# Layer norms of an eight-block network: the scaling of two tiles in every five moves from VectorE to GpSimd

## The chip, the cores and the metric

The kernel runs on one core of a Trainium2 chip, in one launch. The metric is device time in microseconds (us). The engines are TensorE (PE, its weight loads apart as PEld), VectorE (DVE), ScalarE (ACT), GpSimd (POOL) and SyncE (SP), which here issues most DMAs.

## What is computed

A network of eight blocks works on `x`, 128 graphs of 40 nodes with 128 features (5120 rows of 128 numbers, float32). Four blocks work on the graph (a graph convolution or attention within each graph), four are feed-forward (a token mixer with a scan, and three expert layers). Each block is fed with a layer norm of `x`, and its result is added to `x`:

```python
def _layernorm(x, axis=-1, eps=1e-05):
    m = jnp.mean(x, axis=axis, keepdims=True)
    v = jnp.var(x, axis=axis, keepdims=True)
    return (x - m) / jnp.sqrt(v + eps)
...
    x = x + _L1_gnn_ref(_layernorm(x, axis=-1), adj, nodemask, ...)
    x = x + _L1_ffn_ref(_layernorm(x, axis=-1), L1_ffn_gamma, L1_ffn_beta, ...)
```

The second feed-forward block (L1_ffn) takes a layer norm of its own input once more, with a gain and an offset, so there are nine rounds of norm in eight calls.

## The kernel before

`x` is kept turned, as features by rows (`XT`, 128 x 5120). `layer_norm` (line 178) is called eight times, here named by the prefix of its tiles: n0 (before L0_gnn), n1 (L0_ffn), n2 (L1_gnn), n3 (L1_ffn, two rounds), n5 (L2_gnn), n6 (L2_ffn), n7 (L3_gnn), n8 (L3_ffn). A call works on TT = 40 tiles of 128 rows by 128 features and has these steps:

- TensorE turns four tiles at a time into PSUM (`pin`, line 228), ScalarE copies them into `xt` (line 271). n0 and n5 have the rows already.
- VectorE takes `bn_stats` of each tile (`stats`, line 304), then the mean and variance of 20 tiles at once (`moments`, lines 310 to 317). It does so for both halves of 20 tiles before anything else. ScalarE takes the root (`rooted`, line 262).
- `apply` (lines 319 to 330) scales a half: a reciprocal of 128x20 numbers (line 322), a drain, and then 20 instructions `tensor_scalar` on 128x128 numbers (line 328), which subtract the tile's mean and multiply by its reciprocal deviation. Both are pointers to a column of `ms`, one number per row. After every fifth tile it raises `normed`.
- TensorE waits for `normed`, turns five tiles back (`back`, line 236) into one of two PSUM buffers `pout`, and ScalarE copies the 128x640 numbers into `XNP` (line 286, or 288 with gain and offset), then raises `out_copied`.
- With `slots` (n0, n2, n5, n7) TensorE also turns eight pairs of graphs for each five tiles (`turn`, line 247), and ScalarE copies them into `XNG` in two pieces (lines 293 and 296). n1, n3, n6 and n8 have no slots.

With `twice` (n3) the stats and `apply` run once over the raw rows without any of the steps on TensorE, and then again over the result. n3 and n8 also store the normed rows to DRAM (`SparseExperts.store`, `f_xn`, line 892), in two halves, each when `normed` has reached 4 and 8. In n1 the SP queue issues the 26 DMAs for the weights of the next block meanwhile (`load_weights`, line 2583), and GpSimd clears three small tiles. In n2 GpSimd clears some tiles and SP reloads. Otherwise GpSimd has nothing to do within a norm.

Every engine's part of a call is a straight program in order. The call ends with a barrier of all engines (line 184), and the next block's instructions start behind it.

Of the kernel before, what the change touches and what calls it, by code (L numbers as in the profile page):

```python
# [9 lines left out]
ALU = mybir.AluOpType  # L10
# [11 lines left out]
TT = T // 128  # L22
# [155 lines left out]
def layer_norm(nc, g, slots=False, name="ln", tok=None, twice=False, affine=None, ahead=None, keep=None, refresh=False, pads=None):  # L178

    IN, OUT = 4, 5  # L180
    GI, GO = TT // IN, TT // OUT
    HALF = TT // 2
    OB = OUT * 128 // N
    with nc.cleanup_on_exit(), ExitStack() as ctx:
# [4 lines left out]
        if keep is not None:  # L189
            xt, xn = keep.raw, keep.xn  # L190
        else:
            xt = sb("xt", [128, TT, D]) if tok is None else tok
            xn = xt
        turned = tok is None or refresh
        bn, ms, tm = sb("bn", [128, TT, 6]), sb("ms", [128, 2, TT]), sb("tm", [128, 2, TT])
        par = keep.par if keep is not None else sb("par", [128, 2])
        sem = lambda s: nc.alloc_semaphore(f"{name}_{s}")
        par_in, in_ps, copied, var_ready, root, normed, out_ps, out_copied, slot_ps, slot_copied = map(sem, (
            "par_in", "in_ps", "copied", "var_ready", "root", "normed", "out_ps", "out_copied", "slot_ps", "slot_copied"))
        block = ctx.enter_context(nc.Block())  # L200
        ROUNDS = 2 if twice else 1

# [5 lines left out]
        if affine is not None:  # L208
            @block.sync
            def _(sp):  # L210
                for i, p in enumerate(affine):
                    sp.dma_start(par[:, i:i + 1], p.rearrange("(d a) -> d a", a=1), allow_slow_non_contiguous=True).then_inc(par_in, 16)
                if keep is not None:
                    keep.store(sp, normed)
        elif keep is not None:
            @block.sync
            def _(sp):
                keep.store(sp, normed)

        @block.tensor  # L220
        def _(pe):
            if turned:
                for c in range(GI):
                    if c >= 2:
                        pe.wait_ge(copied, c - 1)
                    for k in range(IN):
                        t = IN * c + k
                        mm = pe.transpose(pin[c % 2][:, k, :], xt[:, t, :] if refresh else g.XT[:, t * 128:(t + 1) * 128], g.ident[:])
                    mm.then_inc(in_ps, 1)

            def back(o):
                pe.wait_ge(normed, o + 1)
                if o >= 2:
                    pe.wait_ge(out_copied, o - 1)
                for k in range(OUT):
                    mm = pe.transpose(pout[o % 2][:, k * 128:(k + 1) * 128], xn[:, OUT * o + k, :], g.ident[:])
                mm.then_inc(out_ps, 1)

            def turn(s):
                if pads is not None and s == 0:  # L240
                    pe.wait_ge(pads, 1)
                pe.wait_ge(out_copied, s // 2 + 1)
                if s >= 2:
                    pe.wait_ge(slot_copied, s - 1)
                for q in range(CHP):
                    p = g.XNP[:, s * CHG + 2 * q:s * CHG + 2 * q + 2, :].rearrange("p b n -> p (b n)")
                    mm = pe.transpose(psl[s % 2][:, q, :], p, g.ident[:])
                mm.then_inc(slot_ps, 1)

            for o in range(GO + 1):  # L250
                if o < GO:
                    back(o)
                if slots and o >= 1:
                    turn(2 * o - 2)
                    turn(2 * o - 1)

        @block.scalar
        def _(act):
# [21 lines left out]
            for o in range(GO + 1):  # L280
# [9 lines left out]
                if slots and o >= 1:  # L290
# [4 lines left out]
                    act.wait_ge(slot_ps, s + 1)  # L295
                    act.activation(g.XNG[:, s * CHP:(s + 1) * CHP, :], psl[s % 2][:], ACT.Copy).then_inc(slot_copied, 1)

        @block.vector
        def _(dve):
            def stats(h, fresh, of):  # L300
                for t in range(h * HALF, (h + 1) * HALF):
                    if fresh and t % IN == 0:
                        dve.wait_ge(copied, t // IN + 1)
                    dve.bn_stats(bn[:, t, :], of[:, t, :])
                dve.drain()

            def moments(h):
                c = slice(h * HALF, (h + 1) * HALF)
                f = lambda i: bn[:, c, i]
                dve.tensor_tensor(ms[:, 0, c], f(1), f(4), ALU.add)  # L310
                dve.tensor_tensor(tm[:, 0, c], f(1), f(4), ALU.subtract)
                dve.tensor_tensor(tm[:, 1, c], f(2), f(5), ALU.add)
                dve.drain()
                dve.tensor_scalar(ms[:, 0, c], ms[:, 0, c], 0.5, None, ALU.mult)
                dve.tensor_tensor(tm[:, 0, c], tm[:, 0, c], tm[:, 0, c], ALU.mult)
                dve.drain()
                dve.scalar_tensor_tensor(tm[:, 0, c], tm[:, 1, c], 4.0 / D, tm[:, 0, c], ALU.mult, ALU.add).then_inc(var_ready, 1)

            def apply(r, h):
                c = slice(h * HALF, (h + 1) * HALF)  # L320
                dve.wait_ge(root, 2 * r + h + 1)
                dve.reciprocal(ms[:, 1, c], ms[:, 1, c])
                dve.drain()
                if refresh and h == 0:
                    dve.wait_ge(copied, GI)
                of = xt if r == 0 else xn
                for t in range(h * HALF, (h + 1) * HALF):
                    ins = dve.tensor_scalar(xn[:, t, :], of[:, t, :], ms[:, 0, t:t + 1], ms[:, 1, t:t + 1], ALU.subtract, ALU.mult)
                    if r == ROUNDS - 1 and t % OUT == OUT - 1:
                        ins.then_inc(normed, 1)  # L330

            for r in range(ROUNDS):
                if r:
                    dve.drain()
                of = xt if r == 0 else xn
                stats(0, tok is None and r == 0, of)
                moments(0)
                stats(1, tok is None and r == 0, of)
                moments(1)
                apply(r, 0)  # L340
                apply(r, 1)
# [524 lines left out]
class SparseExperts:  # L866
# [17 lines left out]
        self.w_in, self.stored = sem("w_in"), sem("stored")  # L884
        self.src = (W1, b1, W2, b2)

    def store(self, sp, normed):
        x = self.xn_dram.rearrange("(t p) d -> p t d", p=128)
        for i in range(2):
            cols = slice(i * (TT // 2), (i + 1) * (TT // 2))  # L890
            sp.wait_ge(normed, 4 * i + 4)
            sp.dma_start(x[:, cols, :], self.xn[:, cols, :]).then_inc(self.stored, 16)

    def load(self, sp):
# [417 lines left out]
def l2_gnn(nc, g, adjacency, tok=None):  # L1312
# [3 lines left out]
    with nc.cleanup_on_exit(), ExitStack() as ctx:  # L1316
# [5 lines left out]
        def load_inputs(sp):  # L1322
            sp.dma_start(w[:], g.L2_gnn_W).then_inc(w_in, 16)
            masks = g.nodemask.rearrange("(q j) m -> j q m", j=2)
            for j in range(2):
                sp.dma_start(key[SLOT * j:SLOT * (j + 1), :, :], masks[j][None, :, :].broadcast_to([SLOT, PAIRS, N])).then_inc(key_in, 16)

        layer_norm(nc, g, True, "n5", tok=tok, refresh=tok is not None, ahead={"sync": load_inputs})
        inter = sb("inter", [128, B, N])
        P, hide, st = sb("P", [128, PAIRS, N]), sb("hide", [128, PAIRS, N]), sb("st", [128, PAIRS])  # L1330
# [144 lines left out]
def l3_gnn(nc, g):  # L1475
# [4 lines left out]
    with nc.cleanup_on_exit(), ExitStack() as ctx:  # L1480
# [7 lines left out]
        def load_weights(sp):  # L1488
# [8 lines left out]
            sp.dma_start(fpb[:], g.L3_gnn_fp_b.rearrange("(d a) -> d a", a=1), **slow).then_inc(w_more, 16)  # L1497

        layer_norm(nc, g, True, "n7", ahead={"sync": load_weights})
        wc, wq, wk = sb("wc", [D, HD, D]), sb("wq", [D, HD]), sb("wk", [D, HD])  # L1500
        obias, Q = sb("obias", [D, 1]), sb("Q", [128, PAIRS, HD])
# [1048 lines left out]
def l0_ffn(nc, g, kept):  # L2550


    with nc.cleanup_on_exit(), ExitStack() as ctx:
# [14 lines left out]
        with ExitStack() as first:  # L2568
# [43 lines left out]
            def clear_weights(pool):  # L2612
                pool.memset(raw_dt[:], 0.0).then_inc(ws["z"], 1)
                pool.memset(dtb[:], 0.0).then_inc(ws["z"], 1)
                pool.memset(negA[:], 0.0).then_inc(ws["z"], 1)

            layer_norm(nc, g, False, "n1", ahead={"sync": load_weights, "gpsimd": clear_weights})
            PS = [ctx.enter_context(nc.psum_tensor(f"hy_ps{i}", [128, 512], F32)) for i in range(8)]
            block = first.enter_context(nc.Block())
# [770 lines left out]
```

## Time and profile before

| | |
|---|---|
| median of 3 runs | 3330.44 us (3319.33 to 3331.9) |
| the profiled execution | 3322.45 us, its span 3320.7 us |
| mean granted TensorE clock | 0.85 of full speed |
| busy, share of the span | PE 76%, PEld 48%, DVE 65%, ACT 40%, POOL 22% |

The profile follows one execution. Busy times are sums over the whole span, and say little of a single stage; the timeline gives a row for each instruction or run of like instructions: start, duration, engine, line, operation, names, and in brackets how long the engine had been idle and what released it. The start and end of a row of `x20` are those of the first and the last instruction.

### The profile page before, as it was taken

How to read it: one execution, taken by the hardware profiler on the slowest of the kernel's cores; microseconds unless marked ns; L12 is line 12 of the kernel's file. 1: busy time of each engine (PE TensorE's matmuls, PEld its weight loads, DVE VectorE, ACT ScalarE, POOL GpSimd, SP SyncE). 2: the span in 40 equal slices, each digit the busy share in tenths (PEclk: the TensorE clock that was granted, in tenths of full speed). 3: DMA queues.
4: the chain of work that ended last, by engine and by line, in shares of the span. 5: the costliest groups of instructions: out<-in, count | busy, mean ns of one | idle time of the engine just before them, and what ended most of it. 6: DMA issues, size and time to landing. Idle time of an engine off the chain costs nothing. (4 is left out here: it accounts for less than half of the span.)

```text
span 3320.7 us, 50429 instructions
## 1 busy us (share of the span) xinstructions
PE 2535.9 (76%) x18894; PEld 1605.6 (48%) x18894; DVE 2144.2 (65%) x4297; ACT 1314.4 (40%) x2385; POOL 729.6 (22%) x764
## 2 busy tenths in 40 slices
PE   6477999999999999967258645748849979985740
PEld 5334555555555555535127544624425656652640
DVE  6837887777778888864864778566673357765111
ACT  4333444444444444423337303323314445543640
POOL 0000000000000000000007670037730024310666
PEclk7788999999999999977659756669979979886885
DMA  4311222212222222113113311000012211102332
GB/s 76 113 42 39 52 49 49 49 49 58 59 51 51 49 49 49 46 33 128 41 27 105 65 42 17 1 14 6 6 16 65 63 47 49 41 9 64 89 82 74
DMA packets 177585, 167.48 MB, mean 50 GB/s; under 512 B 82532, under 2 KB 150512, under 8 KB 174664
## 3 DMA queue, kind: packets, MB, share of 16 engines
q1 hardware_dynamic: 156368, 131.86, 15.9%
q0 software_dynamic: 20992, 32.59, 4.7%
q8 instruction: 145, 2.38, 0.3%
q14 instruction: 80, 0.66, 0.1%
HBM read 131.35 MB, written 33.02 MB: 49 GB/s over the span
## 5 line engine op out<-in xcount | busy, mean ns | idle before, releaser
L2887 PE MATMUL hy_ps<-hy_uT,hy_win 128*128 128x512 f32 x1152 | 499.4, 594 | 0.0
L2887 PEld LDWEIGHTS hy_ps<-hy_uT,hy_win 128*128 128x128 f32 x1152 | 217.9, 190 | 283.2 <-issue 271.5
L1827 POOL DMA_DIRECT2D ek_w<-ek_src x32 | 17.9, 561 | 1174.2 <-DVE ek_dst L1849 1174.2
L2949 PE MATMUL hy_ps<-hy_wo,hy_yg 128*128 128x512 f32 x512 | 238.5, 610 | 10.1 <-ACT XNP L3089 8.6
L1146 POOL DMA_INDIRECT f_xg<-f_xn,f_gidx x188 | 178.2, 948 | 131.9 <-POOLq L912 74.9
L1160 POOL DMA_INDIRECT XNP<-f_y,f_pidx x160 | 169.9, 1062 | 76.6 <-issue 48.2
L2390 PE MATMUL er_c<-XNG 128*128 128x400 f32 x480 | 179.6, 531 | 0.0
L1251 DVE TENSOR_TENSOR f_ysl<-f_py,f_cur 128x256 f32<-128x256 f32 x94 | 39.9, 425 | 179.1 <-PE f_py L1187 179.1
L2949 PEld LDWEIGHTS hy_ps<-hy_wo,hy_yg 128*128 128x128 f32 x512 | 93.8, 192 | 120.6 <-issue 98.7
L3168 DVE TENSOR_TENSOR_SCAN XNG<-XNG,hy_fx 128x2048 f32<-128x2048 f32 x32 | 141.6, 4425 | 2.6
L1996 PE MATMUL f_px<-XNG 128*128 128x40 bf16 x736 | 69.1, 266 | 91.0 <-DVE XNG L1948 90.3
L2323 POOL DMA_INDIRECT er_gone<-er_nodes,er_sidx x120 | 123.6, 1030 | 36.6 <-issue 35.0
L2390 PEld LDWEIGHTS er_c<-XNG 128*128 128x128 f32 x480 | 95.2, 204 | 68.0 <-issue 10.8
L855 DVE TENSOR_TENSOR f_hg<-f_hs,f_gb 128x640 f32<-128x640 f32 x64 | 52.7, 825 | 110.0 <-ACT f_hs L837 91.3
L1695 POOL TENSOR_TENSOR g_KB<-g_KB,g_Q 128x1280 f32<-128x1280 f32 x16 | 39.1, 2444 | 376.1 <-DMA g_KB<-g_keys 262.0
L3019 ACT ACTIVATE hy_swT<-hy_ps 64x160 f32<-64x160 f32 x256 | 76.4, 299 | 83.5 <-PE hy_ps L2854 78.6
L1996 PEld LDWEIGHTS f_px<-XNG 128*128 128x128 bf16 x736 | 60.7, 152 | 99.5 <-DVE XNG L1948 99.5
L3119 DVE TENSOR_TENSOR hy_sw<-hy_ps,hy_blg 128x512 f32<-128x512 f32 x64 | 44.3, 692 | 94.0 <-PE hy_ps L2838 94.0
L1187 PEld LDWEIGHTS f_py<-f_cur,f_hT 128*128 128x128 f32 x752 | 99.2, 193 | 5.0
L3089 ACT ACTIVATE XNP<-hy_ps,hy_rms 128x512 f32<-128x512 f32 x64 | 42.2, 681 | 148.9 <-PE hy_ps L2949 148.3
L837 ACT ACTIVATE f_hs<-f_ph,f_b1t 128x320 f32<-128x320 f32 x128 | 67.0, 527 | 84.6 <-PE f_ph L805 84.0
L1179 PE MATMUL f_ph<-f_xT,f_cur 128*128 128x256 f32 x376 | 100.4, 391 | 0.0
(658 smaller groups left out, 6020.9 us busy)
## 6 DMA issues: line engine op xcount, KB each, us to landing
XNG<-hy_decays SPq DMA_DIRECT2D x32, 1024.0 KB, 9.5
hy_rb<-hy_inverse SPq DMA_DIRECT2D x128, 128.0 KB, 3.6
f_y<-f_ysl SPq DMA_DIRECT2D x94, 128.0 KB, 2.0
f_gb<-gate_rows SPq DMA_DIRECT2D x16, 640.0 KB, 5.1
g_KB<-g_keys SPq DMA_DIRECT2D x32, 320.0 KB, 4.4
f_xn<-XNG SPq DMA_DIRECT2D x4, 1280.0 KB
hy_xn<-XNP SPq DMA_DIRECT2D x1, 4096.0 KB, 14.0
hy_XC<-hy_xn SPq DMA_DIRECT2D x16, 256.0 KB
```

What stands on the lines that cost most here:

```text
L837: ins = act.activation(hs[:, e % 2, k, :], psh[e % 2][k][:], ACT.Gelu, bias=b1t[:, e * H2 + k:e * H2 + k + 1])
L1146: pool.indirect_dma_start(out=xg[:, i % NX, h, :], out_offset=None, in_=ex.xn_dram, in_offset=bass.IndirectOffsetOnAxis(ap=ex.gidx[:, n:n ...
L1160: pool.indirect_dma_start(out=yc[:, n % NC_, t, c, :], out_offset=None, in_=ex.y_dram, in_offset=bass.IndirectOffsetOnAxis(ap=ex.pidx[:, n ...
L1179: pe.matmul(psh[i % 2][k], cur[:, i % NW, k * 128:(k + 1) * 128], xT[:, i % 2, :], start=True, stop=True).then_inc(h_ps, 1)
L1187: mm = pe.matmul(psy[i % 2][:, h, :], hT[:, i % 2, k, h * 128:(h + 1) * 128], cur[:, i % NW, H + k * D:H + (k + 1) * D], start=(k == 0), s ...
L1996: mm = pe.matmul(self.ph, self.OL[:, b, :, k], self.OH[:, b, :, k], start=False, stop=False, skip_group_check=True)
L2323: pool.indirect_dma_start(out=gone[:, par, u, :], out_offset=None, in_=tab_dram, in_offset=bass.IndirectOffsetOnAxis(ap=sidx[:, par, u:u + ...
L2390: mm = pe.matmul(flat(acc[j][:]), OD[:, 1 - par, u, j * 128:(j + 1) * 128], flat(X[:, u]), start=False, stop=False, skip_group_check=True)
L2887: mm = pe.matmul(p[:], win[:, t, m * 128:(m + 1) * 128], uT[:, t, :], start=(t == 0), stop=(t == KT - 1))
L2949: mm = pe.matmul(PS[4 + q % 2][:], yg[:, t, q * 128:(q + 1) * 128], wo[:, t, :], start=(t == 0), stop=(t == KT - 1))
L3019: ins = act.activation(o, p[:, :, j, 0:N], ACT.Copy)
L3168: dve.tensor_tensor_scan(L[:, a][:, st], dAb[:, a][:, st], E[:, st], 0.0, ALU.mult, ALU.add)
```

## The change

GpSimd gets a part of each layer norm. Of every five tiles VectorE scales the first three (`BY_DVE = 3`) and GpSimd the last two with the same instruction. VectorE raises `scales` once per half, behind the reciprocal and its drain, and GpSimd waits for it. GpSimd raises `pool_normed` after its second tile of a five, in the last round, and `pool_first` in the round before it. TensorE and the two DRAM stores wait for both `normed` and `pool_normed`; VectorE waits for eight `pool_first` before the stats of the second round of n3.

```diff
@@ layer_norm
+        scales, pool_normed, pool_first = map(sem, ("scales", "pool_normed", "pool_first"))
+        BY_DVE = 3
...
             def back(o):
                 pe.wait_ge(normed, o + 1)
+                pe.wait_ge(pool_normed, o + 1)
...
+        @block.gpsimd
+        def _(pool):
+            for r in range(ROUNDS):
+                of = xt if r == 0 else xn
+                for t in range(TT):
+                    if t % HALF == 0:
+                        pool.wait_ge(scales, 2 * r + t // HALF + 1)
+                    if refresh and t == 0:
+                        pool.wait_ge(copied, GI)
+                    if t % OUT >= BY_DVE:
+                        ins = pool.tensor_scalar(xn[:, t, :], of[:, t, :], ms[:, 0, t:t + 1], ms[:, 1, t:t + 1], ALU.subtract, ALU.mult)
+                    if t % OUT == OUT - 1:
+                        ins.then_inc(pool_normed if r == ROUNDS - 1 else pool_first, 1)
...
                 of = xt if r == 0 else xn
+                dve.sem_inc(scales, 1)
                 for t in range(h * HALF, (h + 1) * HALF):
-                    ins = dve.tensor_scalar(xn[:, t, :], of[:, t, :], ms[:, 0, t:t + 1], ms[:, 1, t:t + 1], ALU.subtract, ALU.mult)
-                    if r == ROUNDS - 1 and t % OUT == OUT - 1:
+                    if t % OUT < BY_DVE:
+                        ins = dve.tensor_scalar(xn[:, t, :], of[:, t, :], ms[:, 0, t:t + 1], ms[:, 1, t:t + 1], ALU.subtract, ALU.mult)
+                    if r == ROUNDS - 1 and t % OUT == BY_DVE - 1:
                         ins.then_inc(normed, 1)
             for r in range(ROUNDS):
                 if r:
+                    dve.wait_ge(pool_first, GO)
                     dve.drain()
@@ SparseExperts.store
             sp.wait_ge(normed, 4 * i + 4)
+            sp.wait_ge(pool_normed, 4 * i + 4)
```

VectorE in n1, before, from the last statistics to the barrier (`n1_ms` are the means and deviations, `n1_xt` the rows):

```order
L317 SCALAR_TENSOR_TENSOR n1_tm<-n1_tm 128x20
L322 RECIPROCAL n1_ms<-n1_ms 128x20 [waits n1_root]
L328 TENSOR_SCALAR n1_xt<-n1_xt,n1_ms 128x128 x20
L322 RECIPROCAL n1_ms<-n1_ms 128x20 [waits n1_root]
L328 TENSOR_SCALAR n1_xt<-n1_xt,n1_ms 128x128 x20
```

and now:

```order
L334 SCALAR_TENSOR_TENSOR n1_tm<-n1_tm 128x20
L339 RECIPROCAL n1_ms<-n1_ms 128x20 [waits n1_root]
L347 TENSOR_SCALAR n1_xt<-n1_xt,n1_ms 128x128 x12
L339 RECIPROCAL n1_ms<-n1_ms 128x20 [waits n1_root]
L347 TENSOR_SCALAR n1_xt<-n1_xt,n1_ms 128x128 x12
```

Eight of the twenty instructions of each half are gone, and the reciprocals stand where they stood.

GpSimd in n1, before, between two barriers:

```order
L2613 MEMSET hy_raw_dt 40x512
L2614 MEMSET hy_dtb 40x1
L2615 MEMSET hy_negA 40x1
L184 UNCONDITIONAL_BRANCH
L184 ISA [waits barrier_Pool_Activation_PE_DVE_SP_gather]
```

and now:

```order
L2634 MEMSET hy_raw_dt 40x512
L2635 MEMSET hy_dtb 40x1
L2636 MEMSET hy_negA 40x1
L301 UNCONDITIONAL_BRANCH
L311 TENSOR_SCALAR n1_xt<-n1_xt,n1_ms 128x128 [waits n1_scales]
L311 TENSOR_SCALAR n1_xt<-n1_xt,n1_ms 128x128 x7
L311 TENSOR_SCALAR n1_xt<-n1_xt,n1_ms 128x128 [waits n1_scales]
L311 TENSOR_SCALAR n1_xt<-n1_xt,n1_ms 128x128 x7
```

Sixteen scalings stand on GpSimd, eight per half, behind the work that it had. In the other seven calls the same sixteen are added, in n3 twice sixteen.

TensorE in n1, now, at the third and fourth five tiles (`n1_o0`, `n1_o1` are the PSUM buffers `pout`):

```order
L239 MATMUL n1_o0<-ident,n1_xt 128x128 [waits n1_out_copied,n1_pool_normed,n1_normed]
L239 MATMUL n1_o0<-ident,n1_xt 128x128 x4
L239 MATMUL n1_o1<-ident,n1_xt 128x128 [waits n1_out_copied,n1_pool_normed,n1_normed]
L239 MATMUL n1_o1<-ident,n1_xt 128x128 x4
L239 MATMUL n1_o0<-ident,n1_xt 128x128 [waits n1_out_copied,n1_pool_normed,n1_normed]
```

The order on TensorE is as before; the wait on `n1_pool_normed` is added.

## Rows read from the trace of the kernel before

**Rows 1.** The page: busy us (share of the span) by engine, and the chain by engine.

```profile
PE 2535.9 (76%) x18894; PEld 1605.6 (48%) x18894; DVE 2144.2 (65%) x4297; ACT 1314.4 (40%) x2385; POOL 729.6 (22%) x764
...
POOL 4%; issue 1%; DMA 1%; PE 0%; DVE 0%; POOLq 0%; DVEq 0%
```

**Rows 2.** Lines 328, 236: duration ns min/median/max; first and last start; who waited, us, times.

```profile
L328 DVE TENSOR_SCALAR n_xt<-n_xt,n_ms x160: 333/342/353, 131.3 to 2684.4; 128x128 f32<-128x128 f32 x160
...
  PEld n_o L236: 96.4, 40
...
L236 PE MATMUL n_o<-ident,xin x40: 272/273/477, 45.3 to 58.1; 128*128 128x128 f32 x40
```

**Rows 3.** Timeline of n8, a norm without slots: start us, us, engine, line.

```profile
2989.66 5.21 DVE L328 TENSOR_SCALAR XNG<-lend,n_ms 128x128 f32<-128x128 f32 x20
...
2991.09 5.17 PE L236 MATMUL n_o<-ident,XNG 128*128 128x128 f32 x20 [5.83 <-DVE XNG L328]
...
3000.41 0.76 PE L236 MATMUL n_o<-ident,XNG 128*128 128x128 f32 x5 [0.52 <-DVE XNG L328]
3001.21 0.70 ACT L286 ACTIVATE XNP<-n_o 128x640 f32<-128x640 f32 x1 [0.57 <-PE n_o L236]
```

**Rows 4.** Timeline of n0, a norm with slots.

```profile
43.84 5.22 DVE L328 TENSOR_SCALAR xin<-xin,n_ms 128x128 f32<-128x128 f32 x20
...
45.26 2.61 PE L236 MATMUL n_o<-ident,xin 128*128 128x128 f32 x10 [13.77 <-DVE xin L328]
...
54.55 0.71 PE L236 MATMUL n_o<-ident,xin 128*128 128x128 f32 x5
...
56.13 0.71 PE L236 MATMUL n_o<-ident,xin 128*128 128x128 f32 x5
```

**Rows 5.** Timeline of n3: the first round's scaling and the second round's start.

```profile
1619.86 5.21 DVE L328 TENSOR_SCALAR XNG<-raw,n_ms 128x128 f32<-128x128 f32 x20
...
1630.62 3.96 DVE L304 BATCH_NORM_STATS2 n_bn<-XNG 128x6 f32<-128x128 f32 x20
...
1652.71 0.89 ACT L288 ACTIVATE XNP<-n_o,f_par 128x640 f32<-128x640 f32 x1 [0.40 <-PE n_o L236]
```

**Rows 6.** GpSimd's one-input instructions: timeline behind n3, and groups with mean ns.

```profile
1654.59 0.29 POOL L955 TENSOR_SCALAR_AFFINE_SELECT f1r_before<-f1r_onesq 128x128 f32<-128x128 f32 x1
1654.85 0.23 POOL L957 IOTA f1r_iob<- 128x128 bf16 x1
...
L132 POOL TENSOR_SCALAR_AFFINE_SELECT a_blk<-a_blk 64x40 f32<-64x40 f32 x2 | 0.5, 233 | 0.1
```

**Rows 7.** VectorE's `tensor_scalar` without and with one pointer: groups with mean ns.

```profile
L1951 DVE TENSOR_SCALAR XNG<-lend 128x4096 f32<-128x4096 f32 x1 | 2.3, 2293 | 0.1
...
L2704 DVE TENSOR_SCALAR hy_bxr<-mean_w,hy_bx 128x128 f32<-128x128 f32 x4 | 1.1, 281 | 0.0
```

**Rows 8.** Timeline in L3_gnn: GpSimd and VectorE beside each other, and GpSimd's instruction alone.

```profile
2708.89 2.88 POOL L1700 TENSOR_TENSOR g_KB<-g_KB,a_adjG 128x1280 f32<-128x1280 f32 x1
...
2754.40 1.49 DVE L1731 TENSOR_TENSOR g_P<-g_P,g_st 128x1280 f32<-128x1280 f32 x1
...
2758.45 2.39 POOL L1695 TENSOR_TENSOR g_KB<-g_KB,g_Q 128x1280 f32<-128x1280 f32 x1 [11.51 <-DVE g_P L1719]
2759.93 2.26 DVE L1725 TENSOR_TENSOR g_P<-g_P,g_st 128x1280 f32<-128x1280 f32 x1
2760.92 4.02 POOL L1700 TENSOR_TENSOR g_KB<-g_KB,a_adjG 128x1280 f32<-128x1280 f32 x1
```

**Rows 9.** Timeline of the end of n1: SP, ScalarE, and the next block's first turns.

```profile
140.44 1.11 SPq L2583 DMA_DIRECT2D hy_sl<-in_L_ffn_W_slice_dram  x2
...
142.81 0.70 ACT L286 ACTIVATE XNP<-n_o 128x640 f32<-128x640 f32 x1 [0.58 <-PE n_o L236]
...
144.62 1.51 PEld L2668 LDWEIGHTS hy_ps<-ident,hy_raw_in 128*128 128x128 f32 x14 [2.09 <-issue]
```

**Rows 10.** The page, DMA issues: the shortest landing (last number, us).

```profile
f_y<-f_ysl SPq DMA_DIRECT2D x94, 128.0 KB, 2.0
```

More of the change, by code:

```diff
@@ L213, in _ @@
                 if keep is not None:
-                    keep.store(sp, normed)
+                    keep.store(sp, normed, pool_normed)
         elif keep is not None:
@@ L217, in _ @@
             def _(sp):
-                keep.store(sp, normed)
+                keep.store(sp, normed, pool_normed)
         @block.tensor
@@ L885, in __init__, with store @@
         self.src = (W1, b1, W2, b2)
-    def store(self, sp, normed):
+    def store(self, sp, normed, pool_normed):
         x = self.xn_dram.rearrange("(t p) d -> p t d", p=128)
```

## Prediction

> **What bounds the kernel now.** I read the page first. It says that no engine is busy for the whole span, that VectorE is busy for 65% of it and GpSimd for 22%; the chain of waits covers only the last tenth of the span and names nothing in a norm [rows 1]. So the shares decide nothing here: the program is a row of stages with a barrier behind each, and the question is what ends last in each of the nine rounds of norm. That is read from the timeline of each.
>
> The work at stake is small. One scaled tile reads 0.342 us, but twenty follow each other in 5.21 us, so the next starts 0.257 us behind, (5.21 - 0.342) / 19 [rows 2, 3]. I call this d. Five tiles, one step for TensorE, take 5d = 1.28 us. There are 9 x 40 = 360 such instructions, 93 us or 2.8% of the span, and all lie where TensorE or nobody else works.
>
> Three kinds of norm differ in what ends last.
>
> - **Without slots (n6, n8, second round of n3, n1).** In n8 TensorE turns five tiles, then waits for the next five until the end: the last five start at 3000.41, after 0.52 us of waiting for VectorE [rows 3]. The whole stretch from the first scaling to the last copy's end is 2989.66 to 3001.91, 12.25 us. VectorE's pace sets it. TensorE could not go much faster at first, though. Its first five turns of a norm run at the low clock: ten turns of n0 take 2.61 us, which is 1.28 until the second five start and 1.33 for those, so with a last turn of 0.477 us (the longest; it is 0.273 once the clock has risen) they follow each other in 0.213 us, and five need 1.07 us [rows 2, 4]. In n8 the first 20 turns are like that.
> - **With slots (n0, n2, n5, n7).** Later fives start 1.58 us apart (54.55, 56.13) with no wait for VectorE [rows 4]: TensorE and ScalarE also do the turns of the slots. VectorE, at 1.28 us, is ahead. It matters only for the first and second five, before which TensorE stands idle.
> - **First round of n3.** VectorE alone: 1619.86 to the next statistics at 1630.62, 10.76 us, with nothing beside it [rows 5].
>
> The sum of TensorE's waits for line 328, 96.4 us in 40 waits [rows 2], is mostly the wait for the statistics before the first five, which the change leaves alone.
>
> **The change, part by part.** (1) VectorE loses 16 scalings of 40 per round: per five it needs 3d = 0.77 us. (2) GpSimd gets these 16; p is the time from one to its next. The trace of before has no `tensor_scalar` on GpSimd. Nearest is its one-input instruction of the same size, 0.29 us long, whose follower starts 0.26 us behind [rows 6]. On VectorE each pointer costs about 0.06 us (343 ns in the mean with two, 281 with one [rows 2, 7]). Lower bound 0.26; with two pointers 0.38. Upper bound from the two-input instruction: 2.88 us for 1280 numbers, 0.29 us for 128, with 0.17 us that is fixed (0.26 less 0.09, below) and 0.12 for the pointers, 0.58 [rows 8]. I take p = 0.38, since the one-input row is nearest. Then GpSimd's two tiles need 0.76 us, just what VectorE's three need, if each ran undisturbed.
>
> (3) Whether they run undisturbed is the real question. In L3_gnn VectorE's instruction, issued at 2759.93, takes 2.26 us where it takes 1.49 alone; it ends at 2762.19, 1.35 us behind the end of GpSimd's at 2760.84. GpSimd's next takes 4.02 us where it takes 2.88 alone [rows 8]. So the two streamed their data strictly one after the other, each waiting for the other's whole instruction, while the fixed parts overlapped (1.35 is less than 1.49, and 4.02 - 2.88 = 1.14 is less than VectorE's 1.27 us that remained). Those have two inputs in SBUF; ours has one. But ours moves two numbers a cycle: 4096 in 2.29 us is 0.56 ns each, against 1.16 ns for the two-input row [rows 8, 7]. The Trainium skill, "SBUF — State Buffer", the section with the single rule on the shared port pair, gives the reason why this speaks against the change: VectorE's single-input instructions reach that rate by taking the second port pair as well, which is GpSimd's only one, as an exclusive lock for the whole instruction. By that rule the two engines' scalings would exclude each other altogether; the trace agrees for two-input instructions, and no row shows it for `tensor_scalar`. By it the sum would be that of the second rival, 11.4 us more, and not the 10.6 us less that follow here.
>
> What must be excluded is only the streaming. VectorE streams a tile in about 0.07 us (128 x 0.56 ns), GpSimd in between 0.09 us (its one-input rows: 292 against 233 ns for 88 numbers more, 0.67 ns each) and 0.29 us. If VectorE is held back by GpSimd's streaming alone, five tiles take G = 0.77 + 2 x 0.09 = 0.95 at least and 0.77 + 2 x 0.29 = 1.35 at most. I take **G = 1.0 us**, near the one-input end, in place of 1.28.
>
> The sum with G = 1.0, 0.28 us per five:
>
> - first round of n3: 8 x 0.28 = 2.2 us off; all of it on the path. The added wait for eight `pool_first` stands where VectorE would start the statistics; it costs only GpSimd's lag.
> - n6, n8, second round of n3: the first five are ready 0.28 earlier, the next three go at TensorE's 1.07 (0.21 off each), and when the clock has risen it catches up: 2.2 us each, 6.6 together. ScalarE's copy in n3 is 0.89 us [rows 5], still under G.
> - n1: capped. SP is at 141.55 with its 26 DMAs, and the next block's turns need the last of them; with the shortest landing in the list of DMA issues, 2.0 us, that is 143.5, and they start at 144.62 now [rows 9, 10]. So 1.1 us off, however fast the norm is.
> - n0, n2, n5, n7: 0.28 for the first five, about 0.1 for the second: 0.4 each, 1.6 us. The rest is hidden by TensorE and ScalarE at 1.58 us, and if that cover were gone each would gain 2.2.
> - waking GpSimd and a wait for the later of two engines, about 0.1 us in each of nine rounds, twice the 0.05 us between VectorE's fifth tile (43.84 + 4 x 0.257 + 0.342 = 45.21) and TensorE's start at 45.26 [rows 4]: 0.9 us added.
> - the two DRAM stores of n3 and n8 go out when eight fives are done, so earlier by the same; nobody waits for them at the barrier. GpSimd's memsets in n1 and n2 end before the statistics do. Both at nothing; if they were late, n2 alone would lose its 0.4 us.
>
> 2.2 + 6.6 + 1.1 + 1.6 - 0.9 = **10.6 us off**. The profiled execution, 3322.45 us, would become 3311.8. It lies 8 us under the median of the three runs, 3330.44, for which I forecast 3319.8, rounded to **3320 us**, 0.3% less. A measurement of this kernel can tell about 0.5%, 16.6 us, from no change, so that this is a forecast of no difference that can be told.
>
> **The rivals.** *No hindrance at all.* Streams of 0.07 and 0.09 us may slip past each other. Then G = 0.77. The first round of n3 gains 8 x 0.51 = 4.1; n6 and n8 about 3.2 each, since TensorE at the low clock holds the first fives at 1.07 and ScalarE the last at 0.70 [rows 3]; the second round of n3 2.8 (copies of 0.89); n1 its 1.1; the slots 0.7 each. 17.2 - 0.9 = 16.3 off, 3314 us. For it: short instructions, long fixed parts. Against: rows 8. This is close to all that this change can give, and it is just under the 0.5%.
>
> *Whole instructions exclude each other.* Then G = 0.77 + 0.76 = 1.53, 0.25 more than now. Per round without slots 8 x 0.25 = 2.0, less 0.3 that GpSimd does during the reciprocal: 1.7, five times (in n1 too, as a longer norm is not capped), 8.5. In the slots 1.53 is under 1.58, so only the first fives are late, 0.5 each, 2.0. With 0.9: 11.4 more, 3342 us. For it: the waits in L3_gnn; against: the fixed parts overlapped there [rows 8]. By the rule on that page of the Trainium skill this is the case.
>
> *GpSimd's tile is dear, and exclusive.* The same mechanism, with p at its upper bound 0.58: G = 1.93. It decides over 0.5% from p = 0.44 on (2p + 0.77 = 1.65: 5 x 2.7 and 4 x 0.7 and 0.9, about 17 us). Then the slots lose their cover, since 1.93 is over 1.58. 5 x (8 x 0.65 - 0.3) = 24.5, 4 x (6 x 0.35 + 0.8) = 11.6, with 0.9 about 37 more, 3367 us. The place is TensorE's wait for `pool_normed` in all norms. For it: GpSimd's two-input row; also VectorE could keep GpSimd waiting for all its twelve tiles of a half, which would start TensorE 2 us or more late in eight calls, about 27 us.
>
> **How the numbers follow.** Forecast (G between 0.95 and 1.35, -12 to +2 us) 0.45; no hindrance 0.15; whole instructions 0.22; dear or starved GpSimd 0.15; left for what I do not see, 0.03. Faster by over 0.5% needs the no-hindrance case with a little luck (or a TensorE clock that rises earlier): 0.07. Slower by over 0.5%: the dear case and a part of the whole-instruction case, 0.17. No difference: 0.76. The range leaves out most of the dear case and the best edge: 3310 to 3346 us, which takes in 3314 and 3342 with some scatter (the three runs differ by 12.6 us).
>
> **What would show it.** VectorE's twelve scalings of a half would read more than 12 x 0.257 + 0.09 = 3.17 us: about 4 by my forecast, 3.17 with no hindrance, 6 with whole exclusion. GpSimd's line 311 gives p. In n8 the distance from the first scaling to the end of the last copy should fall from 12.25 to about 10; the first round of n3 from 10.76 to 8.6; n0's fives should still come 1.58 us apart. The next block behind n1 should start no more than 1.1 us earlier. I am wrong if p is over 0.45 us, if single tiles on VectorE read over 0.6 us, or if TensorE's waits in the norms with slots grow.

## The result and the profile after

The changed kernel takes 3357.13 us in the median of 12 runs (3345.48 to 3367.31). Twelve runs of the kernel before, nine of them new, give 3335.83 us. The ratio is 1.0062, 95% interval 1.0045 to 1.008: the change makes the kernel slower by about 21 us. The profiled execution has a span of 3343.8 us, 23.1 more than before.

The page after, in the line that answers to [rows 1]:

```profile
PE 2553.0 (76%) x18894; PEld 1620.1 (48%) x18894; DVE 2110.2 (63%) x4153; ACT 1314.8 (39%) x2385; POOL 846.6 (25%) x908
```

VectorE has lost 34 us and 144 instructions, GpSimd has gained 117 us and 144 instructions. Moved work costs 3.4 times as much where it went. The instructions by line, after (duration ns min/median/max, first and last start):

```profile
L311 POOL TENSOR_SCALAR n_xt<-n_xt,n_ms x64: 785/814/884, 136.1 to 2701.8; 128x128 f32<-128x128 f32 x64
```

```profile
L347 DVE TENSOR_SCALAR n_xt<-n_xt,n_ms x96: 332/366/432, 136.0 to 2696.3; 128x128 f32<-128x128 f32 x96
```

A tile takes 0.81 us on GpSimd, both by the median reading and by the pace of sixteen (12.90 us). On VectorE it reads 0.366 in the median against 0.342 before [rows 2]: little disturbed. The timeline of n8 after, the norm of [rows 3]:

```profile
3008.68 3.42 DVE L347 TENSOR_SCALAR XNG<-lend,n_ms 128x128 f32<-128x128 f32 x12
3008.69 12.91 POOL L311 TENSOR_SCALAR XNG<-lend,n_ms 128x128 f32<-128x128 f32 x16 [58.31 <-DVEq L340]
...
3012.32 3.27 DVE L347 TENSOR_SCALAR XNG<-lend,n_ms 128x128 f32<-128x128 f32 x12
...
3020.15 1.30 PE L239 MATMUL n_o<-ident,XNG 128*128 128x128 f32 x5 [0.25 <-issue]
...
3021.70 1.30 PE L239 MATMUL n_o<-ident,XNG 128*128 128x128 f32 x5 [0.25 <-issue]
3023.04 0.70 ACT L289 ACTIVATE XNP<-n_o 128x640 f32<-128x640 f32 x1 [0.85 <-PE n_o L239]
3024.49 0.35 SPq L968 DMA_DIRECT2D f3r_wr<-in_L_ffn_Wg_dram  x1
```

VectorE is done at 3015.59, 6.9 us after its start, and GpSimd's sixteen tiles run without a break until 3021.60. The last fives reach TensorE 1.55 us apart (3020.15, 3021.70), two of GpSimd's tiles. The profile puts the wait before them down to "issue", but VectorE has long been done, and each of these two starts 0.10 us behind the end of GpSimd's second tile (3020.05, 3021.60): the wait is for GpSimd.

From the first reciprocal to the next block's first instruction n8 has grown by 2.90 us, in three pieces. The scaling took 10.69 us (2989.66 to 3000.35) and takes 12.91: 2.2. The last five turns take 1.30 us and took 0.76 [rows 3]: 0.54. The rest, 0.14, is three small delays: 0.05 us more before the first scaling, 0.04 between the last one and TensorE, 0.04 behind the last copy. The second piece comes from TensorE's clock. Stretches of n1, second round of n3, n6, n8 and n0, after and before (length, busy time of each engine, granted clock as a share of 2.4 GHz, DMA share, GB/s):

```profile
135.65:151.85 16.20, 10.40 (x40) 7.43 (x40) 7.05 (x27) 5.94 (x9) 12.90 (x16) 0.50 0.33 63
...
1647.68:1664.06 16.38, 10.41 (x40) 7.44 (x40) 7.05 (x27) 7.39 (x9) 12.90 (x16) 0.50 0.40 116
2156.14:2172.47 16.33, 10.40 (x40) 7.43 (x40) 7.05 (x27) 5.94 (x9) 12.90 (x16) 0.50 0.00 1
3008.29:3024.49 16.20, 10.40 (x40) 7.42 (x40) 7.05 (x27) 5.94 (x9) 12.91 (x16) 0.51 0.40 114
43.68:63.75 20.07, 15.64 (x104) 13.97 (x104) 7.05 (x27) 13.77 (x25) 12.90 (x16) 0.78 0.00 1
```

```profile
130.92:144.60 13.68, 7.46 (x40) 5.33 (x40) 10.88 (x43) 5.95 (x9) 0.00 (x0) 0.82 0.40 76
...
1640.81:1654.30 13.49, 8.24 (x40) 5.83 (x40) 10.88 (x43) 7.39 (x9) 0.00 (x0) 0.73 0.45 129
2144.84:2158.16 13.32, 7.43 (x40) 5.30 (x40) 10.89 (x43) 5.95 (x9) 0.00 (x0) 0.81 0.01 2
2989.32:3002.62 13.30, 8.23 (x40) 5.82 (x40) 10.88 (x43) 5.95 (x9) 0.00 (x0) 0.74 0.44 126
43.49:62.38 18.89, 15.30 (x104) 13.46 (x104) 10.90 (x43) 13.57 (x25) 0.00 (x0) 0.81 0.00 1
```

The DVE column has fallen from 10.9 to 7.05 us, the POOL column stands at 12.90 in every stretch. Before, in n1, the second round of n3, n6 and n8, the first two to four fives ran at the lower level of the clock (1.2 GHz, 1.33 us each) and the later ones at the upper (0.76 us each); after the change the clock stays at the lower level through all of them (0.50, 0.51).

Where the time went, norm by norm, in us. Each is measured as for n8; n3a is the first round, up to the reciprocal of the second.

| | n0 | n1 | n2 | n3a | n3b | n5 | n6 | n7 | n8 | sum |
|---|---|---|---|---|---|---|---|---|---|---|
| before | 18.89 | 13.68 | 18.57 | 21.30 | 13.49 | 18.65 | 13.32 | 17.96 | 13.30 | |
| after, more by | 1.18 | 2.52 | 1.28 | 1.99 | 2.89 | 1.20 | 3.01 | 1.98 | 2.90 | 18.95 |

19 of the 23 us lie within the nine rounds; the other 4 are scattered with both signs over stages that the change does not touch (+3.4 us behind n0, -3.2 behind n2).

### The profile page after: what moved, and what is told of

Its sections match the earlier page's. It is cut to its first block and busy times, and to the rows that moved or that the text cites. A ratio compares the mean times of both kernels' runs of the same rounds, so it can differ in the third digit from the quotient of the medians.

```text
span 3343.8 us, 50451 instructions
## 1 busy us (share of the span) xinstructions
PE 2553.0 (76%) x18894; PEld 1620.1 (48%) x18894; DVE 2110.2 (63%) x4153; ACT 1314.8 (39%) x2385; POOL 846.6 (25%) x908
## 5 line engine op out<-in xcount | busy, mean ns | idle before, releaser
L311 POOL TENSOR_SCALAR n_xt<-n_xt,n_ms 128x128 f32<-128x128 f32 x64 | 51.6, 818 | 325.5 <-DVEq L340 325.5
## 6 DMA issues: line engine op xcount, KB each, us to landing
XNG<-hy_decays SPq DMA_DIRECT2D x32, 1024.0 KB, 10.9
```

## The experiments

Theory A after this reading: what a tile costs on GpSimd sets the pace, VectorE hardly disturbs it, and the lost clock adds to that. Sums below are over the nine rounds of each run's trace, against the kernel before.

**The change in the norms with slots alone.**

```diff
-        BY_DVE = 3
+        BY_DVE = 3 if slots else 5
```

with the new waits left out where GpSimd has no share.

> The change made in the four norms with slots alone (n0, n2, n5, n7); the other four calls are as before. The traces of before and after, each norm measured from its first reciprocal to the next block's first instruction, differ by 1.2, 1.3, 1.2 and 2.0 us in these four. Theory A (what GpSimd's tile costs, 0.81 us, sets the pace: five tiles need 1.61 us): 5 to 6 us more than before, ratio about 1.0017, and no difference in n1, n3, n6, n8. Rival B (the loss comes from elsewhere, for instance from GpSimd and VectorE disturbing each other's memory access or from semaphores in every call): the four norms here cost the same as those without slots, some 2.2 us each or more, 9 us or more in all.

Measured: ratio 1.0003, interval 0.9982 to 1.0024. n0, n2, n5, n7 grew by 0.57, 0.29, 0.64 and 1.05 us, 2.6 in all; the others by -0.31 to +0.19. The place is right, and rival B falls, since the cost is far under 2.2 us a norm. The size missed: half of what the same four norms cost in the changed kernel (5.6). Their stretches give a granted clock of 0.81 to 0.84, those of the changed kernel 0.78 to 0.83. The moment at which the clock rises seems to move such a norm by itself: in the next run n0, n2, n5 and n7 are as before the change, and there n5 is 0.73 us shorter, at a clock of 0.90 against 0.82. That is a part of the difference, not shown to be all of it: n5 reads 0.83 both here and in the changed kernel, and is 0.56 us shorter here.

**The change in the norms without slots alone** (`BY_DVE = 5 if slots else 3`).

> The change made in the norms without slots alone (n1, n3 with both its rounds, n6, n8). Theory A: +2.5, +2.0, +2.9, +3.0, +2.9 us, 13.3 us in all, ratio about 1.004. If the whole of the 20 us lies in the norms, this and the run with slots alone add up to 19 us. Rival: a part of the loss (4 us of the traces' difference lies between the norms) belongs to the stages behind a norm, because they start on a TensorE whose clock has stayed low; then this run shows the next blocks behind n1, n3, n6 and n8 longer by 1 us or more each.

Measured: ratio 1.0047, interval 1.002 to 1.0074, about 16 us. The traces have n1 +2.54, n3a +1.99, n3b +3.33, n6 +2.87, n8 +2.90: 13.6 us, where 13.3 was expected, and 13.1 with the untouched norms. The two halves sum to 15.3 us in the traces, and the changed kernel has 19; nearly all of the missing 3.7 lies in the norms with slots, which take 5.6 us more there and 2.0 in the two runs together, and its cause is open, as said above.

By its own sign the rival cannot be dismissed from this trace: the stages behind n1, n3, n6 and n8 are longer by 4.7, 3.2, 2.0 and 1.5 us than before, each over 1 us. But the changed kernel, in which the clock stays as low in these norms, has -0.5, +0.6, +1.2 and +1.2 there, and the run with four tiles on VectorE, in which the clock rises as before, has +1.8, +2.9, +2.8 and +2.7. So these stages are longer whatever the clock did in the norm ahead of them, and the rival finds no support. The trace of the kernel before (3322.45 us, with a median of 3335.83) is a short one, and a difference of a few us outside the norms says nothing. Most of the loss is in the norms where TensorE has nothing but the five turns to do.

**Four tiles for VectorE, one for GpSimd** (`BY_DVE = 4`).

> VectorE scales four of five tiles and GpSimd one (BY_DVE = 4). Theory A: GpSimd's one tile takes 0.81 to 0.87 us, under VectorE's four at 4 x 0.257 + 0.06 to 0.1 = 1.09 to 1.13 us, so five tiles need 1.1 in place of 1.28 us: the first round of n3 falls from 11.1 to about 9.9 us (first reciprocal to next statistics), n6 and n8 gain about 1 to 1.5 us, the whole kernel some 5 to 8 us (ratio about 0.998). Rival B (the two engines exclude each other for whole instructions): five tiles need 4 x 0.257 + 0.81 = 1.84 us, and the kernel is slower than the changed one. Rival C (the fixed cost of a second engine in each call decides): no faster than before although GpSimd is never waited for.

Measured: 3328.96 us against 3335.57 before, ratio 0.9979, interval 0.9955 to 1.0003. In the trace all nine rounds are shorter, 9.3 us in all; n3a by 1.93 (1.2 expected), n6 by 1.46, n8 by 1.57. Its n8:

```profile
2992.86 4.36 DVE L347 TENSOR_SCALAR XNG<-lend,n_ms 128x128 f32<-128x128 f32 x16
2992.88 3.33 POOL L311 TENSOR_SCALAR XNG<-lend,n_ms 128x128 f32<-128x128 f32 x4 [56.19 <-DVEq L340]
...
3001.94 0.77 PE L239 MATMUL n_o<-ident,XNG 128*128 128x128 f32 x5 [0.17 <-DVE XNG L347]
```

VectorE needs 4.36 us for 16 tiles, so 1.07 to 1.09 for four, and GpSimd is done first (3.33 us for its four of a half). If whole instructions excluded each other, four fives could not take less than 16 x 0.257 + 4 x 0.78 = 7.2 us. That rules out rival B, and the gain rules out C. Waiting for a second engine is cheap; what decides is which of the two ends last.

**TensorE turns each five twice** in the changed kernel.

```diff
-                for k in range(OUT):
+                for k in list(range(OUT)) * 2:
                     mm = pe.transpose(pout
```

> The changed kernel with each five tiles turned twice on TensorE in the back step (the same result is written again), so that TensorE has twice the work there. In the traces TensorE's granted clock is 0.50 through all of n1, n3, n6 and n8 after the change, and 0.74 to 0.82 on average before; the last five turns then take 1.30 in place of 0.76 us. Theory A with the clock as its second part: with more turns the clock rises within n6 and n8 (mean over 0.6), the last turns of a five read 0.71 to 0.77, and n8 is no more than 0.3 us longer than after the change for twice the turns at its end. Rival (the clock has nothing to do with how busy TensorE was): the clock stays at 0.50, ten turns need 2.1 us per five, and n6 and n8 grow by 4 us or more.

Measured: n8 takes 16.18 us, after the change 16.20. Its last ten turns, in the timeline:

```profile
3060.24 1.28 PE L239 MATMUL n_o<-ident,XNG 128*128 128x128 f32 x10 [0.27 <-issue]
```

Its stretch, with the columns of the stretches above:

```profile
3046.83:3063.01 16.18, 11.93 (x80) 11.22 (x80) 7.06 (x27) 5.94 (x9) 12.91 (x16) 0.79 0.40 113
```

Twice the turns, a clock of 0.79 in place of 0.51, and the last ten turns take 1.28 us where the last five took 1.30. n1, the second round of n3 and n6 read 0.81, 0.84 and 0.75, and last 16.19, 16.37 and 16.19 us, against 16.20, 16.38 and 16.33. So the clock follows the turns here: with nothing changed but their number it comes back, at the same pace of GpSimd's. What differs between before and the changed kernel is that the same turns come 1.55 to 1.67 us apart in place of 1.28, so that TensorE stands idle for 0.25 to 0.38 us between two fives, where before, in n8, the first twenty turns ran as one row of 5.17 us [rows 3]. The low clock costs no pace there, since even at 1.2 GHz five turns take 1.07 us of the 1.55 to 1.67 between two fives; it costs the 0.5 us of the last five, once per norm. The norms with slots, where TensorE has little room, grew by 3.6 to 4.4 us.

**What makes a tile dear on GpSimd.** Five kernels change only GpSimd's instruction. Each of them, like the kernel with double turns, ran once, so their traces are read and not their times:

```diff
-  pool.tensor_scalar(xn[:, t, :], of[:, t, :], ms[:, 0, t:t + 1], ms[:, 1, t:t + 1], ALU.subtract, ALU.mult)
+  pool.tensor_scalar(xn[:, t, :], of[:, t, :], 0.0, 1.0, ALU.subtract, ALU.mult)
```

> GpSimd's tiles are scaled by the immediates 0.0 and 1.0 in place of the two pointers into the means and deviations, so two of five tiles are left unnormed. It shows what the pointers cost on GpSimd. My split of the 0.79 us that a tile takes on GpSimd alone: 0.17 fixed, 0.27 for 128 numbers at the two-input rows' rate, and so 0.17 for each pointer. Theory A (pointers are dear on GpSimd): about 0.45 us a tile, and five tiles fall under 1.28 us, so that n8 is shorter than before. Rival B (the numbers are dear, or the fixed part is): 0.7 us or more.

```diff
+  pool.tensor_scalar(xn[:, t, 0:64], of[:, t, 0:64], ms[:, 0, t:t + 1], ms[:, 1, t:t + 1], ALU.subtract, ALU.mult)
```

> GpSimd scales only the first 64 of the 128 columns of its tiles, with its pointers (the other 64 are left unnormed). Theory A: half of the numbers saves 0.13 us, a tile takes about 0.66 us. Rival B (the numbers are dear, 0.6 us for 128): about 0.5 us.

```diff
+  pool.tensor_scalar(xn[:, t, :], of[:, t, :], ms[:, 0, t:t + 1], 1.0, ALU.subtract, ALU.mult)
```

> GpSimd's tiles subtract the mean by pointer but multiply by the immediate 1.0 (these tiles are left unscaled). Theory A: half way between the two pointers and none, 0.62 us a tile. Rival B: the first pointer costs nearly all, or nothing.

```diff
+  pool.tensor_scalar(xn[:, t:t + 2, :], of[:, t:t + 2, :], 0.0, 1.0, ALU.subtract, ALU.mult)   # once per five
```

> GpSimd treats its two tiles of a five in one instruction of 256 columns with the immediates 0.0 and 1.0 (they are left unnormed). With the run of immediates on 128 columns it parts the fixed cost from that of the numbers. Theory A: 0.17 fixed and 0.27 per 128 numbers, so 0.71 us for the two tiles. Rival B (a large fixed part): under 0.6 us, little more than one tile with immediates.

and one operation:

```diff
+  pool.tensor_scalar(xn[:, t, :], of[:, t, :], 0.0, None, ALU.subtract)
```

> GpSimd's tiles get one operation with an immediate (subtract 0.0) in place of two with immediates, so two of five tiles are left unnormed. The run of two immediates took 0.61 us from tile to tile, and 3.3 us per thousand columns (0.63 us at 128, 1.06 at 256). Theory A: the second operation costs, per number, so one takes about half, 0.4 us a tile. Rival B (the rate is that of any tensor_scalar on GpSimd): 0.6 us as before.

GpSimd's instructions in n0 of these, one fence per kernel, in the order immediates, half width, one pointer, wide, one operation (ns min/median/max):

```profile
L311 POOL TENSOR_SCALAR xin<-xin x16: 632/632/655, 44.6 to 53.8; 128x128 f32<-128x128 f32 x16
```

```profile
L311 POOL TENSOR_SCALAR xin<-xin,n_ms x16: 579/694/862, 44.4 to 54.1; 128x64 f32<-128x64 f32 x16
```

```profile
L311 POOL TENSOR_SCALAR xin<-xin,n_ms x16: 708/736/791, 44.5 to 55.5; 128x128 f32<-128x128 f32 x16
```

```profile
L311 POOL TENSOR_SCALAR xin<-xin x8: 1062/1134/1194, 44.3 to 52.1; 128x256 f32<-128x256 f32 x8
```

```profile
L311 POOL TENSOR_SCALAR xin<-xin x16: 519/536/546, 44.1 to 51.7; 128x128 f32<-128x128 f32 x16
```

The last instructions of n0, with VectorE idle, read within 10 ns of these minima; the changed kernel's minimum is 785. They fit one sum. From 128 to 256 columns 1062 - 632 = 430 ns, 3.4 ns a column; from 64 to 128 columns with pointers 785 - 579 = 206, 3.2 ns, which is the one check that the sum was not fitted to. The first pointer adds 708 - 632 = 76, the second 785 - 708 = 77. Fixed: 632 - 430 = 202. So the tile's 0.79 us are 0.20 fixed, 0.43 for 128 numbers through two operations, and 0.15 for the pointers. My split (0.17, 0.27, 0.34) had the sum right, as it was fitted to it, and two parts wrong: the run of immediates read 0.63 in place of 0.45. A second operation is part of it: one reads 519, 113 ns less, 18% of the 632, not half.

None of the five expectations had the size. The immediates read 0.63 where A said 0.45 and B 0.7 or more, though n8 is shorter than before, as A had it; half the width 0.58, between 0.66 and 0.5; one pointer 0.71 where 0.62 was expected, though half way between two and none, as A had it; the wide form 1.06 where A said 0.71 and B under 0.6; one operation 0.52, between 0.4 and 0.6.

What VectorE does meanwhile matters too, and by the form. With 64 columns GpSimd's tiles follow each other in 0.56 us alone and in about 0.70 beside VectorE, single ones reading up to 0.86. With immediates GpSimd keeps its 0.61 us beside VectorE, and VectorE's twelve tiles take 3.76 us in n8 in place of 3.17.

Their rounds follow the pace. The immediates leave 0.61 us from tile to tile (9.79 us for 16), five tiles in 1.22, and n8 is 0.82 us shorter than before, all nine rounds 5.5. At 0.65 us a tile (half width) the nine rounds are 1.8 us shorter, at 0.73 (one pointer) 7.1 longer, at 0.51 (one operation) 13.9 shorter; the wide form, 1.10 us for two tiles, is 9.2 shorter. The point where two of five on GpSimd neither gain nor lose is near 0.64 us a tile, half of 1.28.

**The four-to-one split once more.**

> The same kernel as e3_four_one, to narrow its ratio, whose interval was 0.9955 to 1.0003. The norms of its trace are 9.3 us shorter than before in all, 0.28%. Theory A: ratio 0.997 to 0.998 again, norms 8.5 to 10 us shorter. Rival C: the gain was scatter, ratio 1.000.

Measured: 3332.52 us against 3341.53, ratio 0.9978, interval 0.9959 to 0.9997; norms 11.2 us shorter, more than the 8.5 to 10 expected. The two traces are of the same kernel, and differ most in n0 (18.56 and 17.69 us, at a clock of 0.82 and 0.86) and n5 (18.62 and 17.68, at 0.82 and 0.90). With the first measurement this is a gain of 0.2%, small, but this time with an interval that does not reach 1. Of the splits of this work it is the one that beats both kernels.

## Why the prediction was wrong

I forecast 10.6 us off and no difference that can be told; it was 21 us on, past the high end of the range, on the side to which I had given 0.17. Of the 37 us between 3320 and 3357, 11 are the gain that did not come, 21 the loss that did, and 5 the three runs of the kernel before, whose median lay that much under the median of twelve.

- **The bounding of the norms** was right: where VectorE's pace ruled before, in the four norms without slots and the first round of n3, GpSimd's rules now, and 13.3 of the 19 us lie there. With slots the fives still come 1.57 us apart late in n0 (57.47 and 59.04), as before [rows 4].
- **Step (2), p, failed.** I took 0.38 us and let it go to 0.58; from one tile to the next it is 0.78 undisturbed (12.90 / 16 = 0.81 on average). That alone turns the sign: GpSimd's two tiles need 1.61 us, not 0.76, against the 1.28 of before. The nearest row was no guide. Its slope of 0.67 ns a number [rows 6] became 3.4 for `tensor_scalar`, five times as much, and more than the 2.25 of the two-input row [rows 8] that I held for an upper bound. The pointers, priced at 0.06 us from VectorE, cost 0.077.
- **Step (3), G,** was asked the wrong way round. VectorE's twelve tiles take 3.42 us beside GpSimd and would take 3.17 alone, and GpSimd's read 0.83 to 0.88 beside VectorE, 0.79 alone. In this form the two hinder each other by some 0.06 us per GpSimd tile, near the 0.09 of my forecast. But with p = 0.81 the fives wait for GpSimd alone, G = 2p = 1.61, so that neither 2p + 0.77 nor 0.77 plus the streams counts. The "SBUF — State Buffer" page of the Trainium skill, in its section "Who interferes with whom", has whole instructions exclude each other when VectorE's `tensor_scalar` runs in its two-port mode, which with this p would be G = 2.4; the trace disagrees, for these instructions of 128 columns, if VectorE's was in that mode. No row shows the mode. With one pointer VectorE passes 512 columns in 482 ns (line 2705 of the kernel before), more than one number in each 1.16 ns of the two-input row; the rows with two pointers have 128 columns.
- **The rival "dear and exclusive"** had the sign and half the mechanism. Its threshold, p over 0.44, assumed exclusion. Without it, two of five decide from 0.64, and by 5 x (8 x 0.33 - 0.3) = 11.7 for the rounds without slots; measured 13.3. With slots G = 1.61 lies just over the 1.58 of TensorE and ScalarE, by the same working 4 x (6 x 0.03 + 0.66) = 3.4 us; 5.6 in the changed kernel, 2.6 with the change in these norms alone.
- **The clock** was a term put at nothing: I let it rise on the way, as before, and took it into no sum. At G = 1.61 it does not rise in n1, n3, n6 and n8, and the last five turns cost 0.54 us more in each: 2.2 us.
- **n1's cap** by SP's DMAs was never reached, as the norm became longer. In the four-to-one run n1 is 1.9 us shorter than before, and the next block's turns start at 142.49, 1.42 us behind SP's last issue (141.07), where I had put 2.0: the cap of 1.1 us was too tight.

The signs that I had named did tell it at once: line 311 over 0.45 us, n8 at 15.06 us from the first scaling to the end of the last copy, where I expected about 10, and VectorE's half at 3.42, by my list nearer "no hindrance" than the forecast.

## What to carry to other kernels

Before work is given to another engine, find its price there for that very operation; an instruction of the same shape and another kind can be off by five times. Share tiles by price: with 0.26 against 0.81 us three to one is even, so one of five gains and two of five lose. Where TensorE is fed in small portions, look at its granted clock too: here slower feeding kept it down and made the last portion 0.54 us longer.

## What the hardware showed that I had not expected

- `tensor_scalar` on GpSimd, float32, two operations: 202 ns and 3.4 ns per column, 77 ns for each pointer scalar; with one operation 519 ns for 128 columns.
- GpSimd and VectorE scale tiles in SBUF side by side with little loss: 12 VectorE tiles in 3.42 us against 3.17, GpSimd's 0.79 us to between 0.83 and 0.88. With immediates on GpSimd it is VectorE that waits (3.76 us for 12 tiles in n8), and GpSimd reads 0.63 to 0.66; with 64 columns it is GpSimd (about 0.70 us a tile against 0.56).
- In n8, with a five every 1.6 us, the granted clock stays at 1.2 GHz (0.51); with each five turned twice at the same pace the stretch reads 0.79. What remains open is when exactly it rises in the norms with slots, two of which differ by 0.9 us between two traces of the same kernel.
